# Masked graph attention: who issues the loads of the adjacency

## The chip, the cores and the metric

The kernel runs on one core of a Trainium2 chip. The metric is the device time of one execution in microseconds; lower is better. Where several runs are given, the median counts.

## The reference

With M = N = 6144 rows and D = 128:

```python
h = jnp.maximum(_layernorm(x, axis=-1), 0.0)
scores = jnp.where(adj > 0, h @ weight @ input.T, -2 ** 32 + 1)      # 6144 x 6144
out = x + softmax(scores / 0.07, axis=1) @ input
```

`adj` is a 6144 x 6144 int32 matrix of zeros and ones, 151 MB, and by far the largest input. The scores are wanted at nearly fp32 precision, so operands are split into a high and a low fp16 half.

## The kernel before

**Tiles and chunks.** The 6144 rows are worked on in 48 tiles of 128 rows. A tile's row of scores has 6144 columns. TensorE makes it in six chunks of 1024 columns (`score`, L816 to L824: six matmuls of 512 columns each, 36 per tile). VectorE masks each chunk with the codes of the adjacency (`mask`, L625 to L635), two chunks to each buffer of `codes`.

**The adjacency.** A tile's 128 x 6144 integers come in three loads of 128 x 2048 (1 MB each) into the three buffers of `adj_i`. GpSimd turns each buffer into codes by one pass (`convert`, L419 to L426): it waits for the load (`adj_in[c]`), and until the masks of the previous tile have read the buffer of `codes` that it will write (`masked`), and its end increments `coded`. The load of the next tile into the same buffer of `adj_i` may go out as soon as that pass has read it. SyncE issues it, after a wait on `coded`: `early_adj` (L317 to L322, L340) for tiles 1 and 2, and `next_adj` (L343 to L346) three times in each tile's step for tile t + 3. All of SyncE's transfers are on one DMA queue.

**The other things on SyncE.** In each tile's step SyncE also issues three pairs of transposes (`turn_d`, L324 to L336) that turn half of the exponentials, split by VectorE and ScalarE into fp16 halves, into `pT_dma`, from which TensorE multiplies (L859, L865, L867). A transpose waits for VectorE's `turn_freed` and for the product that last read its buffer. Then there are one load of x for the layernorm, one transpose of h (L368, after a wait on `h_split_done`), and one load of x for the residual. The order of these in a step is written out by hand, `next_adj(0)` behind the pair of c = 2, `next_adj(1)` behind the pair of c = 4, `next_adj(2)` behind the next tile's first pair.

**TensorE.** In a tile's step (L944 to L963) it runs three cycles; each turns two blocks of 512 columns through PSUM (`turn`, eight matmuls), makes two chunks of scores for tiles ahead, and multiplies four blocks of 512 with v (`product`, L848 to L869: eight matmuls each). The first tile's products wait for the low half of v, in four parts: block k needs part k // 3 (L850).

**GpSimd.** Its order is written out too: h of tiles 0 and 1; then, in the head (L453 to L466), the passes of tiles 0 to 2, mixed with the four parts of the low half of v (`v_lo_pool`, L428 to L437) and h of tile 2. In each tile's step t (L468 to L483): the pass for chunk 1 of tile t + 2, h of tile t + 3 and its split, the pass for chunk 2 of tile t + 2 and the one for chunk 0 of tile t + 3.

The steps of tiles 0 to 2 and of the last five are written out, the others are a loop over two tiles (`steps`, L287 to L295).

Of the kernel before, what the change touches and what calls it, by code (L numbers as in the profile page):

```python
# [5 lines left out]
def gnn_masked_attention_kernel(  # L6
# [93 lines left out]
    with ctx:  # L100
# [6 lines left out]
        def sem(name):  # L107
            return ctx.enter_context(nc.semaphore(name))
# [68 lines left out]
        x_ln_in = [sem(f"x_ln_in{i}") for i in range(2)]  # L177
        x_res_in = [sem(f"x_res_in{i}") for i in range(2)]
        adj_in = [sem(f"adj_in{i}") for i in range(CONVS)]
        stored = [sem(f"stored{i}") for i in range(2)]  # L180
        ident_zero = sem("ident_zero")
        ident_done = sem("ident_done")
# [116 lines left out]
        @block.sync  # L299
        def _(sp):  # L300
            def load_x(u, s):
                sp.dma_start(x_ln[:, s, :], x_v[u]).then_inc(x_ln_in[s], 16)

            def load_adj(u, c):
                sp.dma_start(adj_i[:, c, :], adj_v[u][:, c * CONV:(c + 1) * CONV]).then_inc(adj_in[c], 16)

            sp.dma_start(w[:, :], weight).then_inc(w_in, 16)
            for i in range(NODE_PARTS):
                blocks = slice(i * NODE_PART, (i + 1) * NODE_PART)
                sp.dma_start(nodes_raw[:, blocks, :], nodes_v[i]).then_inc(nodes_in[i], 16)  # L310
            for c in range(CONVS):
                load_adj(0, c)
            sp.dma_start(x_res[:, 0, :], x_v[0]).then_inc(x_res_in[0], 16)
            for u in range(2, 4):
                sp.wait_ge(h_done, u - 1)
                load_x(u, u % 2)
            def early_adj(n):  # L317
                sp.wait_ge(coded, n + 1)
                load_adj(n // CONVS + 1, n % CONVS)

            for n in range(2 * CONVS - 1):
                early_adj(n)  # L322

            def turn_d(u, c, g, count):  # L324
                d = c + g
                if count is None:
                    sp.wait_ge(split_done, d // 2 + 1)
                else:
                    sp.wait_ge(turn_freed, count)
                sp.sem_inc(sp_waited, 1)  # L330
                if not (isinstance(u, int) and u == 0):

                    sp.wait_ge(pv_done, u * TURNS + (2 * c + g + 1 - TURNS))
                sp.sem_inc(sp_waited, 1)
                sp.dma_start_transpose(pT_dma[:, d, :, :], split[:, d, :, :].rearrange("p s n -> p (s n)"))\  # L335
                    .then_inc(turned_in[d], 16)  # L336

            for g in range(2):
                turn_d(0, 0, g, g + 1)
            early_adj(2 * CONVS - 1)  # L340

            def step(t, par, at):
                def next_adj(c):  # L343
                    if has(at, 3):
                        sp.wait_ge(coded, t * CONVS + (2 * CONVS + c + 1))
                        load_adj(t + 3, c)  # L346

                for g in range(2):
                    turn_d(t, 2, g, late(at, 0, g) if at == LAST else evac(t, g - 2))
                next_adj(0)  # L350
                for g in range(2):
                    turn_d(t, 4, g, late(at, 1, g) if at == LAST else evac(t, 2 + g))
                next_adj(1)
                if has(at, 4):
                    sp.wait_ge(h_done, t + 3)
                    load_x(t + 4, par)
                if has(at, 1):
                    for g in range(2):
                        turn_d(t + 1, 0, g, late(at, 2, g) if at == LAST - 1 else evac(t, 6 + g))
                next_adj(2)  # L360
                if has(at, 3):

                    sp.wait_ge(scores_made, t * SCORES + 2 * SCORES)
                    sp.sem_inc(sp_waited, 1)
                    sp.wait_ge(h_split_done, t + (4 - H_TENSOR))
                    sp.sem_inc(sp_waited, 1)
                    s = 1 - par
                    sp.dma_start_transpose(hT[:, s, :, :], h_split[:, s, :, :].rearrange("p s n -> p (s n)"))\  # L368
                        .then_inc(hT_in[s], 16)
                if has(at, 1):  # L370
                    if at != 0:
                        sp.wait_ge(fin_done, t)
                    s = 1 - par
                    sp.dma_start(x_res[:, s, :], x_v[t + 1]).then_inc(x_res_in[s], 16)

            steps(sp, step)

        @block.gpsimd
        def _(pool):
# [37 lines left out]
                    .then_inc(h_split_done, 1)  # L417

            def convert(u, c):  # L419
                pool.wait_ge(adj_in[c], u * 16 + 16)  # L420
                if not (isinstance(u, int) and u == 0):

                    pool.wait_ge(masked, u * SCORES + (PER_CONV * (c + 1) - SCORES))
                pool.sem_inc(pool_waited, 1)
                nc.gpsimd.tensor_scalar(codes[:, c, :], adj_i[:, c, :], PRESENT_STEP, ABSENT, ALU.mult, ALU.add)\  # L425
                    .then_inc(coded, 1)  # L426

            def v_lo_pool(i):  # L428

# [578 lines left out]
```

## Time and profile before

| | us |
|---|---|
| median of 3 runs | 922.92 |
| lowest and highest | 921.91, 924.13 |
| the profiled execution, its time | 925.21 |
| its span in the profile | 923.4 |
| TensorE busy (PE) | 904.7, 98% |
| VectorE busy (DVE) | 809.6, 88% |
| ScalarE busy (ACT) | 738.4, 80% |
| GpSimd busy (POOL) | 419.4, 45% |
| granted TensorE clock, mean | 1.00 |
| moved by DMA | 242.46 MB, 263 GB/s |

Busy time is the union of the spans of an engine's instructions; matmul ends are modelled, so a busy TensorE need not be at its peak. The issuing of a transfer isn't counted as busy; such instructions are shown on the issuing engine's queue (SPq for SyncE, POOLq for GpSimd). An idle time in square brackets stands with what ended it.

### The profile page before, as it was taken

Reading aid. Unit: us, or ns where it says so; the run is one execution under the profiler, and the core shown is the slowest. Engines: PE = TensorE matmul, PEld = TensorE weight load, DVE = VectorE, ACT = ScalarE, POOL = GpSimd, SP = SyncE. Lnnn points to the kernel's source line nnn. Section 1 sums busy time; section 2 is a strip of 40 time slices with the busy share of each in tenths; the row PEclk is TensorE's granted clock in tenths of the full one; section 3 lists DMA queues with packets and bytes.
Section 4 is the critical chain, followed back from the end, with each engine's and each line's share of the span. In section 5 each row is a group of like instructions: output and inputs, shape, how many; then the busy total and the mean of one; then the engine's idle time right before and its main releaser. Section 6 shows DMA issues by size and latency. Waiting matters only on the chain.

```text
span 923.4 us, 25567 instructions
## 1 busy us (share of the span) xinstructions
PE 904.7 (98%) x7566; PEld 658.0 (71%) x7566; DVE 809.6 (88%) x1623; ACT 738.4 (80%) x1465; POOL 419.4 (45%) x447
## 2 busy tenths in 40 slices
PE   7999989999999999999999999999999999999997
PEld 4466767777777777777777777777777777777776
DVE  6988878988998899889988998898889888989985
ACT  5877778888888888888888888888888888888885
POOL 3974434444444444434543454445444544444402
DMA  9799999999999999999999999999999999999965
GB/s 317 242 252 282 272 229 273 283 267 277 274 271 264 279 273 272 263 275 274 273 270 267 274 275 274 271 266 273 275 275 259 275 276 276 260 275 270 272 108 100
DMA packets 364969, 242.46 MB, mean 263 GB/s; under 512 B 321808, under 2 KB 346512, under 8 KB 346512
## 3 DMA queue, kind: packets, MB, share of 16 engines
q1 hardware_dynamic: 357744, 238.87, 101.5%
q10 hardware_dynamic: 7200, 3.28, 1.4%
q8 instruction: 13, 0.21, 0.1%
q14 instruction: 12, 0.10, 0.1%
HBM read 160.50 MB, written 3.15 MB: 177 GB/s over the span
## 4 chain that ended last, share of the span: by engine, by line
PE 89%; DMA 4%; DVE 3%; SPq 2%; issue 1%; ACT 0%; DVEq 0%; ACTq 0%
PE ps_s L821 37%; PE ps_o L865 26%; PE ps_o L867 13%; PE ps_t L844 13%; DMA pT_dma<-split 3%; SPq L335 1%; DVE probs L631 1%; DMA nodes_raw<-in_L_gnn_input_dram 1%; SPq L310 1%; PE ps_t L884 1%; DVE split L660 0%; DVE pT_lo L654 0%; PE ps_o L884 0%; ACT yT_hi L544 0%; DVE pT_hi L650 0%
## 5 line engine op out<-in xcount | busy, mean ns | idle before, releaser
L425 POOL TENSOR_SCALAR codes<-adj_i 128x2048 uint32<-128x2048 int32 x144 | 273.8, 1902 | 292.7 <-DVE chunk_max L631 271.6
L631 DVE CUSTOM_DVE_ANT_0 probs<-ps_s,codes 128x1024 f32<-128x1024 f32 x288 | 351.5, 1221 | 50.2 <-PE ps_s L821 42.8
L821 PE MATMUL ps_s<-yT_hi,hT 128*128 128x512 f16 x1152 | 389.2, 379 | 0.9 <-DVE chunk_max L631 0.9
L539 ACT ACTIVATE pT_hi<-ps_t 128x512 f16<-128x512 f32 x281 | 167.8, 597 | 159.5 <-PE ps_t L844 159.4
L865 PE MATMUL ps_o<-v,pT_dma 128*128 128x256 f16 x1152 | 221.0, 273 | 6.7 <-DMA pT_dma<-split 6.7
L509 ACT ACTIVATE ps_t<-probs,neg_max,exp_scale 128x512 f32<-128x512 f32 x285 | 220.3, 773 | 5.3 <-DVE neg_max L641 4.0
L821 PE MATMUL ps_s<-yT_lo,hT 128*128 128x512 f16 x576 | 218.3, 379 | 0.0
L654 DVE TENSOR_TENSOR pT_lo<-ps_t,pT_hi 128x512 f16<-128x512 f32 x284 | 194.5, 685 | 26.1 <-ACT pT_hi L539 24.6
L865 PE MATMUL ps_o<-v,pT_hi 128*128 128x256 f16 x1152 | 205.8, 273 | 0.8 <-DVE pT_lo L654 0.8
L867 PE MATMUL ps_o<-v,pT_dma 128*128 128x128 f16 x1152 | 205.6, 219 | 0.0
L867 PE MATMUL ps_o<-v,pT_lo 128*128 128x128 f16 x1152 | 198.0, 219 | 0.0
L821 PEld LDWEIGHTS ps_s<-yT_hi,hT 128*128 128x128 f16 x1152 | 112.8, 98 | 107.9 <-DVE chunk_max L631 2.5
L660 DVE TENSOR_TENSOR split<-ps_t,split 128x512 f16<-128x512 f32 x285 | 182.5, 681 | 1.6 <-ACT split L519 1.5
L498 ACT ACTIVATE probs<-probs,neg_max,exp_scale 128x1024 f32<-128x1024 f32 x144 | 177.3, 1231 | 0.0
L844 PE MATMUL ps_t<-ident,probs 128*128 128x128 f32 x1136 | 172.3, 274 | 1.2 <-DVE split L660 1.1
L519 ACT ACTIVATE split<-ps_t 128x512 f16<-128x512 f32 x285 | 151.6, 581 | 0.0
L865 PEld LDWEIGHTS ps_o<-v,pT_dma 128*128 128x128 f16 x1152 | 112.6, 98 | 36.2 <-DMA pT_dma<-split 8.1
L865 PEld LDWEIGHTS ps_o<-v,pT_hi 128*128 128x128 f16 x1152 | 112.7, 98 | 29.2 <-DVE pT_lo L654 1.3
L867 PEld LDWEIGHTS ps_o<-v,pT_dma 128*128 128x128 f16 x1152 | 112.6, 98 | 17.1
L867 PEld LDWEIGHTS ps_o<-v,pT_lo 128*128 128x128 f16 x1152 | 112.7, 98 | 16.3
L844 PEld LDWEIGHTS ps_t<-ident,probs 128*128 128x128 f32 x1136 | 119.4, 140 | 5.3 <-DVE split L660 1.6
L821 PEld LDWEIGHTS ps_s<-yT_lo,hT 128*128 128x128 f16 x576 | 56.4, 98 | 36.9 <-issue 1.3
(78 smaller groups left out, 444.4 us busy)
## 6 DMA issues: line engine op xcount, KB each, us to landing
adj_i<-in_adj_dram SPq DMA_DIRECT2D x144, 1024.0 KB, 5.3
pT_dma<-split SPq DMA_TRANSPOSE x288, 3.5
nodes_raw<-in_L_gnn_input_dram SPq DMA_DIRECT2D x6, 512.0 KB, 7.1
x_res<-in_x_dram SPq DMA_DIRECT2D x48, 64.0 KB, 4.0
out_dram<-fin ACTq DMA_DIRECT2D x48, 64.0 KB, 2.6
x_ln<-in_x_dram SPq DMA_DIRECT2D x46, 64.0 KB, 4.9
hT<-h_split SPq DMA_TRANSPOSE x45, 5.1
x_ln<-in_x_dram ACTq DMA_DIRECT2D x2, 64.0 KB, 3.1
```

The costliest lines, as they stand in the source:

```text
L425: nc.gpsimd.tensor_scalar(codes[:, c, :], adj_i[:, c, :], PRESENT_STEP, ABSENT, ALU.mult, ALU.add)\
L498: nc.scalar.activation(part, part, ACT.Exp, bias=neg_max[:, s, :], scale=exp_scale[:, :], accum_out=chunk_sum[:, s, c // 2:c // 2 + 1]).th ...
L509: nc.scalar.activation(part if n is None else ps_t[n % BANKS][:, :], part, ACT.Exp, bias=neg_max[:, s, :], scale=exp_scale[:, :], accum_ou ...
L519: nc.scalar.activation(split[:, d, 0, :], ps_t[n % BANKS][:, :], ACT.Copy)\
L539: nc.scalar.activation(pT_hi[:, p % BANKS, :], turn_area(k, at), ACT.Copy).then_inc(hi_done, 1)
L631: nc.vector.tensor_tensor_reduce(out=probs[:, s, j * SCORE:(j + 1) * SCORE], in0=ps_s[j % 2][:, :], in1=codes[:, c, part * SCORE:(part + 1 ...
L654: nc.vector.tensor_tensor(pT_lo[:, p % BANKS, :], area, pT_hi[:, p % BANKS, :], ALU.subtract)\
L660: nc.vector.tensor_tensor(split[:, d, 1, :], ps_t[n % BANKS][:, :], split[:, d, 0, :], ALU.subtract).then_inc(turn_freed, 1)
L821: made = nc.tensor.matmul(ps_s[j % 2][:, q * 512:(q + 1) * 512], hT[:, s, part, :], y[:, cols], start=(part == 0 and y is yT_hi), stop=(pa ...
L844: made = nc.tensor.transpose(area[:, b * P:(b + 1) * P], probs[:, par, col:col + P], ident[:, :])
L865: nc.tensor.matmul(area[:, 0:2 * D], hi[b], v[:, blk, :, :].rearrange("p s d -> p (s d)"), start=(blk == 0), stop=(k == final and b == PER ...
L867: made = nc.tensor.matmul(area[:, 0:D], lo[b], v[:, blk, 0, :], start=False, stop=(k == final and b == PER_TURN - 1), skip_group_check=True)
```

## The change

GpSimd issues the load of the next tile's chunk itself, directly behind the pass that has read the buffer, after a wait until that pass has ended. SyncE issues only the three loads of tile 0, and its waits on `coded` are gone with the others. The loads that GpSimd issues have semaphores of their own (`adj_pool_in`), on which the passes of tiles 1 to 47 wait. The order of the rest is the same on both engines.

```diff
@@ GpSimd @@
             def convert(u, c):
-                pool.wait_ge(adj_in[c], u * 16 + 16)
+                if isinstance(u, int) and u == 0:
+                    pool.wait_ge(adj_in[c], 16)
+                else:
+                    pool.wait_ge(adj_pool_in[c], u * 16)
                 if not (isinstance(u, int) and u == 0):
 
                     pool.wait_ge(masked, u * SCORES + (PER_CONV * (c + 1) - SCORES))
                 pool.sem_inc(pool_waited, 1)
                 nc.gpsimd.tensor_scalar(codes[:, c, :], adj_i[:, c, :], PRESENT_STEP, ABSENT, ALU.mult, ALU.add)\
                     .then_inc(coded, 1)
+                if not (isinstance(u, int) and u + 1 >= TILES):
+
+                    pool.wait_ge(coded, u * CONVS + (c + 1))
+                    pool.sem_inc(pool_waited, 1)
+                    nc.gpsimd.dma_start(adj_i[:, c, :], adj_v[u + 1][:, c * CONV:(c + 1) * CONV])\
+                        .then_inc(adj_pool_in[c], 16)
@@ SyncE @@
-            def early_adj(n):
-                sp.wait_ge(coded, n + 1)
-                load_adj(n // CONVS + 1, n % CONVS)
-
-            for n in range(2 * CONVS - 1):
-                early_adj(n)
-
...
             for g in range(2):
                 turn_d(0, 0, g, g + 1)
-            early_adj(2 * CONVS - 1)
 
             def step(t, par, at):
-                def next_adj(c):
-                    if has(at, 3):
-                        sp.wait_ge(coded, t * CONVS + (2 * CONVS + c + 1))
-                        load_adj(t + 3, c)
-
                 for g in range(2):
                     turn_d(t, 2, g, late(at, 0, g) if at == LAST else evac(t, g - 2))
-                next_adj(0)
                 for g in range(2):
                     turn_d(t, 4, g, late(at, 1, g) if at == LAST else evac(t, 2 + g))
-                next_adj(1)
...
-                next_adj(2)
```

## Rows read from the trace of the kernel before

**Rows 1.** The page, part 1: busy time, share of the span, instructions.

```profile
PE 904.7 (98%) x7566; PEld 658.0 (71%) x7566; DVE 809.6 (88%) x1623; ACT 738.4 (80%) x1465; POOL 419.4 (45%) x447
```

**Rows 2.** Busy time by stretches of the span, with TensorE's granted clock and DMA.

```profile
core 0: us, PE busy (x) PEld busy (x) DVE busy (x) ACT busy (x) POOL busy (x), PEclk, DMA share, GB/s
...
20.00:40.00 20.00, 19.38 (x73) 7.86 (x72) 18.70 (x37) 15.15 (x21) 19.00 (x11) 1.00 0.70 261
40.00:60.00 20.00, 18.24 (x144) 12.19 (x143) 17.10 (x33) 16.50 (x35) 18.51 (x16) 1.00 1.08 268
...
80.00:100.00 20.00, 19.22 (x166) 13.95 (x164) 17.07 (x34) 15.53 (x32) 8.27 (x9) 1.00 1.19 262
...
300.00:500.00 200.00, 200.00 (x1701) 146.86 (x1700) 179.00 (x361) 163.89 (x329) 90.48 (x99) 1.00 1.05 272
...
900.00:923.40 23.40, 17.23 (x188) 15.11 (x186) 13.65 (x28) 13.59 (x28) 5.34 (x6) 1.00 0.52 99
```

**Rows 3.** Waits, whole span: waiter, releaser; us in total, times, longest us.

```profile
PE ps_o L865 <- DMA pT_dma<-split: 6.7, 7, 1.7
...
POOL h L404 <- POOL h_centred L397: 9.9, 48, 0.2
```

**Rows 4.** Timeline of TensorE: start us, us, instruction, [idle before, releaser].

```profile
57.48 0.27 PE L865 MATMUL ps_o<-v,pT_dma 128*128 128x256 f16 x1 [1.00 <-DMA pT_dma<-split]
...
58.58 0.27 PE L865 MATMUL ps_o<-v,pT_dma 128*128 128x256 f16 x1
...
70.03 0.28 PE L865 MATMUL ps_o<-v,pT_dma 128*128 128x256 f16 x1 [0.17 <-DMA pT_dma<-split]
...
84.32 0.28 PE L865 MATMUL ps_o<-v,pT_dma 128*128 128x256 f16 x1 [0.78 <-DMA pT_dma<-split]
...
127.62 0.28 PE L865 MATMUL ps_o<-v,pT_dma 128*128 128x256 f16 x1 [1.11 <-DMA pT_dma<-split]
...
135.65 0.28 PE L865 MATMUL ps_o<-v,pT_dma 128*128 128x256 f16 x1 [1.74 <-DMA pT_dma<-split]
```

**Rows 5.** Timeline of GpSimd in the head.

```profile
19.69 1.90 POOL L425 TENSOR_SCALAR codes<-adj_i 128x2048 uint32<-128x2048 int32 x1 [0.59 <-DMA adj_i<-in_adj_dram]
22.27 1.90 POOL L425 TENSOR_SCALAR codes<-adj_i 128x2048 uint32<-128x2048 int32 x1 [0.67 <-DMA adj_i<-in_adj_dram]
...
51.74 3.11 POOL L436 TENSOR_TENSOR v<-nodes_raw,v 128x1536 f16<-128x1536 f32 x1
```

**Rows 6.** Instructions of the tiles adj_i and pT_dma: ns min/median/max, first and last start.

```profile
L305 SPq DMA_DIRECT2D adj_i<-in_adj_dram x144: 328/367/1737, 9.0 to 872.4; - x144
L425 POOL TENSOR_SCALAR codes<-adj_i x144: 1897/1901/1925, 17.2 to 880.5; 128x2048 uint32<-128x2048 int32 x144
...
L335 SPq DMA_TRANSPOSE pT_dma<-split x288: 1231/1237/4418, 40.2 to 914.4; - x144
```

**Rows 7.** Timeline of GpSimd in the steady part.

```profile
507.43 1.90 POOL L425 TENSOR_SCALAR codes<-adj_i 128x2048 uint32<-128x2048 int32 x1 [4.22 <-DVE chunk_max L631]
...
515.72 1.90 POOL L425 TENSOR_SCALAR codes<-adj_i 128x2048 uint32<-128x2048 int32 x1
519.66 1.90 POOL L425 TENSOR_SCALAR codes<-adj_i 128x2048 uint32<-128x2048 int32 x1 [2.04 <-DVE chunk_max L631]
```

**Rows 8.** Timeline of SyncE's queue, at 126 us and in the steady part.

```profile
126.10 7.51 SPq L335 DMA_TRANSPOSE pT_dma<-split  x2
...
508.87 2.84 SPq L335 DMA_TRANSPOSE pT_dma<-split  x2
512.02 0.45 SPq L305 DMA_DIRECT2D adj_i<-in_adj_dram  x1
```

**Rows 9.** Timeline of TensorE in the steady part.

```profile
514.82 0.27 PE L865 MATMUL ps_o<-v,pT_dma 128*128 128x256 f16 x1
```

**Rows 10.** The page, parts 5 (groups) and 6 (issues: KB each, us to landing).

```profile
L631 DVE CUSTOM_DVE_ANT_0 probs<-ps_s,codes 128x1024 f32<-128x1024 f32 x288 | 351.5, 1221 | 50.2 <-PE ps_s L821 42.8
...
adj_i<-in_adj_dram SPq DMA_DIRECT2D x144, 1024.0 KB, 5.3
pT_dma<-split SPq DMA_TRANSPOSE x288, 3.5
```

More of the change, by code:

```diff
@@ L179, in gnn_masked_attention_kernel @@
         adj_in = [sem(f"adj_in{i}") for i in range(CONVS)]
+        adj_pool_in = [sem(f"adj_pool_in{i}") for i in range(CONVS)]
         stored = [sem(f"stored{i}") for i in range(2)]
```

## The prediction

> **What bounds the kernel now.** I read the busy table first: TensorE is at work for 904.7 of 923.4 us [rows 1]. The table by stretches then says where the other 18.7 us lie: from 300 to 500 us TensorE is busy for all of 200.00 us, at full granted clock, and the missing time is at the two ends [rows 2]. So in the steady part, nothing that the change does can gain; it can only lose there, by making TensorE wait. The gain can come from the first 140 us or the last 25. The waits name the candidate: TensorE waited 6.7 us in seven pieces for the transposes that SyncE issues (pT_dma) [rows 3]. Five of them are in the timeline: 1.00 us at 57.48, 0.17 at 70.03, 0.78 at 84.32, 1.11 at 127.62, 1.74 at 135.65 [rows 4]; the other two lie ahead of the first of these, and at the end of the run, when no adjacency is loaded any more.
>
> The second reading is the engine that gets the new work. Over the whole run GpSimd is only 45% busy [rows 1], which looks harmless. By stretches it is not: 19.00 of 20 us from 20 to 40, 18.51 of 20 from 40 to 60, and then 90.48 of 200 [rows 2]. In the head it has the passes of three tiles and the low halves of v to make, back to back, and it has 8.27 us of work from 80 to 100. An average would have hidden this.
>
> **The change, part by part.**
>
> *SyncE gives up 141 loads and their waits.* An issue there takes 0.37 us [rows 6], so some 1.1 us per tile come off its queue, together with its waits on `coded`. In the steady part this is worth nothing: its transposes wait for VectorE's split. The other effect is in the queue. SyncE's loads and transposes share one queue, and where a load has just gone in, the transposes behind it are slow: the pair at 126.10 took 7.51 us to issue, where an undisturbed one takes 2.84 [rows 8]. Off that queue, the 0.17 and 0.78 us at 70 and 84 us should go, 0.95 us. The waits at 127.62 and 135.65, 2.85 us together, come around that one long pair; the profile doesn't say whether the load ahead is its whole cause, and I count half, 1.4 us. The 1.00 us at 57.48 vanishes behind the delay worked out below. Gain: 2.4 us, with bounds of 0 and 3.8.
>
> *GpSimd gets, behind each pass with a next tile, a wait on its own pass and an issue.* The wait is the kind it already has: 9.9 us over 48 in `h`, 0.2 us each [rows 3]. The issue has no row, since GpSimd issues no transfer now. The nearest rows are SyncE's: 0.37 us for the very same load, and 1.24 us for a transpose, the longest issue there when nothing stands in its way [rows 6]. The bounds are 0.37 below and, above, one of GpSimd's own passes over a megabyte, 1.90 us [rows 6]. I take 1.24: the load's own row is another engine's, and between ends so far apart the value in the middle has a row of its own. With the wait that is 1.44 us for each pass.
>
> The Trainium skill speaks against the move in "DMA: Bandwidth & Descriptors", section "Specifications": a transfer issued by GpSimd takes about 1 us to its first byte, because a program writes its descriptors, and one from SyncE about 0.6 us. No row here shows it; taking 1.0 us for the issue instead of 1.24 would make the head's cost, worked out next, 4.6 us instead of 6.5.
>
> *What it costs in the head.* What waits for GpSimd there is, in order, the codes of tiles 0 to 2, h of tile 2, and the four parts of the low half of v. The tightest is the last part of v: GpSimd finishes it at 51.74 + 3.11 = 54.85 us [rows 5], and the first product that needs it, k = 9 of tile 0, starts at 58.58 [rows 4], so there are 3.73 us in hand. In GpSimd's order eight passes stand ahead of it (tile 0's three, tile 1's three, the first two of tile 2), each with an issue behind it now. GpSimd was idle before two of them, 0.59 and 0.67 us, waiting for tile 0's loads [rows 5], and that takes up 1.26 us. So the part comes 8 x 1.44 - 1.26 = 10.3 us later, at 65.1, and the product 10.3 - 3.73 = 6.5 us later. The earlier gates (codes of tile 1, h of tile 2, the third part of v for k = 6) are late by less and are steps on the way to the same 65.1, not additions. Behind it TensorE has nothing idle that could take the delay up [rows 2], so the whole run moves by it. SyncE, in its turn, is held by `h_split` of tile 3, which comes about 10 us later than before, and so reaches its next transposes about when their data is ready, since that has also moved by 6.5 us; I price that at nothing, and its cover is the same delay.
>
> *In the steady part GpSimd's extra work is covered.* A tile has 156 matmuls (36 for scores, 96 for products, 24 turns), and 1701 are in those 200 us [rows 2], so a tile takes 200 x 156 / 1701 = 18.3 us. Of that GpSimd is busy 90.48 x 18.3 / 200 = 8.3 us, and three issues with their waits add 3 x 1.44 = 4.3. The only two passes close together start at 515.72 and 519.66; the first ends at 517.62, its issue would at 519.06, and 2.04 us of idle time stood there [rows 7]. If the issue took over 1.8 us the second would slip a little, and its codes are for the next tile's step, at least a third of a tile (6 us) later. Cost: nothing.
>
> *The loads themselves move.* In the steady part, SyncE issues a load only after the transposes that stand ahead of it: the pass that starts at 507.43 ends at 509.33 [rows 7], but the load goes out at 512.02, behind the pair of 508.87 [rows 8]. Now it will go out at about 509.5 and flow from about 510.8, beside the second transpose. A load takes 5.3 us to land and a transpose 3.5 [rows 10]. This pair is used from 514.82 on [rows 9], 2.45 us after the first lands; the second is used one product and one turn, 1.1 us, later. I take zero, with the next rival as the upper end.
>
> Sum: +6.5 - 2.4 = +4.1 us. The profiled execution took 925.21 us (span 923.42); the median is 922.92, 0.25% below it. On the median this gives 927.0 us. A measurement of this kernel can tell about 0.2%, 1.85 us, from no change.
>
> **Rivals.**
>
> *The issue is cheap.* At 0.37 us, 8 x 0.57 - 1.26 = 3.3 us, less than the 3.73 in hand, so the head loses nothing. Then only the gain is left: 2.4 us, 920.5, at best 3.8, and 919.1. The two signs meet at about 0.62 + 2.4 / 8 = 0.92 us per pass, wait included. For it: SyncE does the same load in 0.37. Against it: it is another engine. Chance 0.22, of which a tenth ends within the 0.2%.
>
> *The steady part takes a new wait.* If a load that flows beside a transpose holds it up by its own full length, about 3 us, the pair at 508.87 comes 0.5 us too late for 514.82. At most two of the three pairs per tile can lie so, since GpSimd's passes and the pairs are spread differently over the tile. Where one of them stalls TensorE by 0.2 us in each of 44 tiles, the run gets 9 us longer, and 936 comes out. For it: 7.51 us for a pair in trouble [rows 8]. Against it: sharing is likely fairer than that, and the second transpose's later use. The point from which it decides is a delay of about 2.5 us. Chance 0.12. It makes the run slower on top of the head.
>
> *GpSimd is kept from its issue by VectorE.* If each issue had to sit out one of VectorE's long operations, 1.22 us [rows 10], a pass would cost 1.44 + 1.22 = 2.66 us and the head 8 x 2.66 - 5.0 = 16.3 us: about 937 with the gain. The operation reads one operand from PSUM (ps_s) and one from SBUF (codes) [rows 10]. The Trainium skill, "SBUF — State Buffer", section "Who interferes with whom", has this rule: GpSimd cannot write its descriptors while VectorE runs in a mode that takes both ports. By the same section an operation with one SBUF operand outside those modes does not take them, and no run here has tried it. Chance 0.05.
>
> *The change does nothing measurable,* because the issue's price falls between 0.6 and 0.9 us, and the head's loss and the queue's gain cancel: 8 x 0.8 - 5.0 - 2.4 = -1.0 to 8 x 1.1 - 5.0 - 2.4 = +1.4 us, or 921.9 to 924.3. Chance 0.10.
>
> **How the numbers follow.** The forecast, head later by 3 to 12 us, has 0.51; cheap issue 0.22; cancelled 0.10; steady wait 0.12; ports 0.05. Faster: 0.20. Within 0.2%: 0.02 + 0.10 and a little of the forecast's lower edge, 0.13. Slower: 0.67. The forecast's own range is the issue at 0.9 to 1.9 us: 8 x 2.1 - 5.0 = 11.8 us with no gain gives 934.7, 8 x 1.1 - 5.0 = 3.8 less the full 3.8 gives 922.9. For 8 in 10 the range must take in most of the cheap case and part of the steady wait: 919.5 to 936.
>
> **What would show it.** Right: GpSimd issues of about 1.2 us behind each pass; the last part of v done at about 65 us; TensorE idle for some 6 us between 40 and 60, ended by GpSimd's v or codes; the later waits for pT_dma shorter; full 200 of 200 us from 300 to 500. Wrong: the part of v done before 58 us, or an issue under 0.6 us; TensorE short of 200 us in the steady stretch with pT_dma as the releaser; or waits at 127 and 135 us that stay whole.

## The result, and the profile after

The changed kernel takes **1119.85 us** (median of 7 runs, 1107.76 to 1152.23), the kernel before 921.91 us beside it (7 runs, 921.13 to 924.13): a ratio of 1.209 (95% interval 1.207 to 1.211). Ratios here and below leave out runs more than 1.5% above the fastest of their kernel (here 1140.66 and 1152.23 us), so they can lie below the quotient of the medians (here 1.215), and where too few runs are left none is given. The forecast of 927.0 us had the direction and not the size; 1119.85 lies far outside 919.5 to 936. The profiled execution took 1152.23 us, span 1150.5, the longest of the seven: its rows say where the time goes, not to the microsecond how much.

The page, part 1 (columns as in [rows 1]), and from part 3 the queues: SyncE's is q1, GpSimd's q0 (packets, MB, share of the 16 engines' time).

```profile
PE 966.7 (84%) x7566; PEld 678.3 (59%) x7566; DVE 812.1 (71%) x1623; ACT 738.6 (64%) x1465; POOL 502.9 (44%) x588
...
q1 hardware_dynamic: 337440, 91.01, 54.3%
q0 software_dynamic: 20304, 147.86, 42.8%
```

VectorE and ScalarE are busy for as long as before. They, and TensorE, wait. Busy time by stretches, which answers [rows 2]:

```profile
core 0: us, PE busy (x) PEld busy (x) DVE busy (x) ACT busy (x) POOL busy (x), PEclk, DMA share, GB/s
20.00:40.00 20.00, 19.37 (x72) 7.78 (x71) 18.71 (x36) 15.15 (x21) 17.86 (x12) 1.00 0.70 243
40.00:60.00 20.00, 13.55 (x81) 8.12 (x78) 11.54 (x22) 10.79 (x23) 16.67 (x15) 0.83 1.05 184
80.00:100.00 20.00, 11.34 (x67) 7.36 (x66) 7.54 (x17) 4.97 (x10) 5.30 (x9) 0.66 0.94 170
300.00:500.00 200.00, 168.56 (x1334) 119.16 (x1335) 138.21 (x277) 127.46 (x256) 82.80 (x98) 0.93 1.00 211
500.00:700.00 200.00, 173.82 (x1397) 122.89 (x1395) 147.36 (x294) 134.10 (x268) 90.33 (x108) 0.96 0.99 223
```

TensorE is no longer full in the steady part: 168.56 of 200 us, and 1334 matmuls instead of 1701. A tile of 156 matmuls now takes 200 x 156 / 1334 = 23.4 us, where it took 18.3. Five microseconds a tile over some 44 tiles is 220 us, nearly all of the 227 us that the profiled execution lost. The DMA engines count as busy as before and move 211 instead of 272 GB/s. The waits, which answer [rows 3] (waiter, releaser; us in total, times, longest):

```profile
PE ps_o L859 <- DMA pT_dma<-split: 170.3, 64, 10.2
...
POOL adj_i L419 <- POOL codes L413: 98.9, 138, 0.8
```

Of TensorE's 6.7 us for the transposes 170.3 have become. The groups of the page (parts 5 and 6) and the transposes' row, beside [rows 6, 10]:

```profile
L419 POOL DMA_DIRECT2D adj_i<-in_adj_dram x141 | 84.3, 598 | 103.6 <-POOL codes L413 98.9
...
adj_i<-in_adj_dram POOLq DMA_DIRECT2D x141, 1024.0 KB, 7.2
pT_dma<-split SPq DMA_TRANSPOSE x288, 5.1
```

```profile
L329 SPq DMA_TRANSPOSE pT_dma<-split x288: 1230/1248/10650, 40.4 to 1141.5; - x144
```

The issue by GpSimd costs 0.60 us, and the wait for its own pass 98.9 / 138 = 0.72 us. A load takes 7.2 us to land instead of 5.3, a transpose 5.1 instead of 3.5, and a single transpose's issue up to 10.65. The timeline of the head and of one steady pair (the SPq row at 502.63 holds two pairs, the second from 508.45 on):

```profile
19.96 0.78 POOL L419 DMA_DIRECT2D adj_i<-in_adj_dram  x1 [0.67 <-DMA adj_i<-in_adj_dram]
...
49.88 0.37 PE L859 MATMUL ps_o<-v,pT_dma 128*128 128x256 f16 x1 [4.27 <-DMA pT_dma<-split]
...
61.12 3.09 POOL L430 TENSOR_TENSOR v<-nodes_raw,v 128x1536 f16<-128x1536 f32 x1
...
64.70 0.10 PEld L859 LDWEIGHTS ps_o<-v,pT_dma 128*128 128x128 f16 x1 [5.24 <-POOL v L430]
...
501.15 1.89 POOL L413 TENSOR_SCALAR codes<-adj_i 128x2048 uint32<-128x2048 int32 x1 [2.92 <-DVE chunk_max L625]
502.63 11.16 SPq L329 DMA_TRANSPOSE pT_dma<-split  x4
503.77 0.58 POOL L419 DMA_DIRECT2D adj_i<-in_adj_dram  x1 [0.73 <-POOL codes L413]
...
513.54 0.39 PE L859 MATMUL ps_o<-v,pT_dma 128*128 128x256 f16 x1 [3.75 <-DMA pT_dma<-split]
```

In the head the product comes as late as forecast: the last part of v ends at 61.12 + 3.09 = 64.21 us (forecast 65.1), and the product that needs it starts at 64.73 instead of 58.58, 6.15 us later (forecast 6.5). But v isn't all that it waited for. The chain (the page's part 4, in order of time) reaches it through one transpose, issued at 46.28 and landed at 64.59, 0.4 us after v:

```profile
46.28 18.31 DMA pT_dma<-split
```

So the product would have come as late with v ready in time. TensorE had waited 4.27 us for another transpose at 49.88 already, and it goes on losing behind the head's passes (11.34 of 20 us busy from 80 to 100, before 19.22). The steady part isn't as forecast at all: the first transpose of a pair goes in at 502.63, GpSimd's load 1.1 us behind it, and the second transpose at 504.45; in the chain that one takes 9.04 us, and TensorE's wait of 3.75 us at 513.54 ends with it:

```profile
504.45 9.04 DMA pT_dma<-split
```

### The profile page after: what moved, and what is told of

Read it like the earlier page. It is cut to its first block, busy times and chain, and to the rows that moved or that the text cites. A ratio compares the mean times of both kernels' runs of the same rounds, so it can differ in the third digit from the quotient of the medians.

```text
span 1150.5 us, 25730 instructions
## 1 busy us (share of the span) xinstructions
PE 966.7 (84%) x7566; PEld 678.3 (59%) x7566; DVE 812.1 (71%) x1623; ACT 738.6 (64%) x1465; POOL 502.9 (44%) x588
## 4 chain that ended last, share of the span: by engine, by line
PE 39%; DMA 39%; issue 6%; SPq 6%; DVE 6%; POOL 2%; DVEq 1%; ACT 0%; POOLq 0%
DMA pT_dma<-split 38%; PE ps_s L815 18%; PE ps_o L859 12%; PE ps_o L861 5%; SPq L329 5%; PE ps_t L838 4%; DVE split L654 3%; DVE fin_a L671 1%; DVE probs L625 1%; POOL codes L413 1%; DMA adj_i<-in_adj_dram 1%; SPq L311 1%; POOL v L430 1%; DVE pT_lo L648 0%; DVE fin L677 0%
## 5 line engine op out<-in xcount | busy, mean ns | idle before, releaser
L815 PE MATMUL ps_s<-yT_hi,hT 128*128 128x512 f16 x1152 | 409.6, 397 | 2.0 <-DVE chunk_max L625 2.0
L859 PE MATMUL ps_o<-v,pT_dma 128*128 128x256 f16 x1152 | 232.1, 282 | 170.5 <-DMA pT_dma<-split 170.3
L859 PEld LDWEIGHTS ps_o<-v,pT_dma 128*128 128x128 f16 x1152 | 115.5, 100 | 216.9 <-DMA pT_dma<-split 169.0
L815 PE MATMUL ps_s<-yT_lo,hT 128*128 128x512 f16 x576 | 229.6, 399 | 0.0
L859 PE MATMUL ps_o<-v,pT_hi 128*128 128x256 f16 x1152 | 218.7, 283 | 0.8 <-DVE pT_lo L648 0.8
L861 PE MATMUL ps_o<-v,pT_dma 128*128 128x128 f16 x1152 | 215.6, 225 | 0.0
L861 PE MATMUL ps_o<-v,pT_lo 128*128 128x128 f16 x1152 | 208.5, 225 | 0.0
L859 PEld LDWEIGHTS ps_o<-v,pT_hi 128*128 128x128 f16 x1152 | 117.8, 102 | 36.7 <-issue 5.8
L419 POOL DMA_DIRECT2D adj_i<-in_adj_dram x141 | 84.3, 598 | 103.6 <-POOL codes L413 98.9
L861 PEld LDWEIGHTS ps_o<-v,pT_lo 128*128 128x128 f16 x1152 | 117.3, 102 | 19.3 <-issue 5.2
L861 PEld LDWEIGHTS ps_o<-v,pT_dma 128*128 128x128 f16 x1152 | 115.9, 101 | 16.5
```

Of the source, the lines that this page charges most:

```text
L815: made = nc.tensor.matmul(ps_s[j % 2][:, q * 512:(q + 1) * 512], hT[:, s, part, :], y[:, cols], start=(part == 0 and y is yT_hi), stop=(pa ...
L859: nc.tensor.matmul(area[:, 0:2 * D], hi[b], v[:, blk, :, :].rearrange("p s d -> p (s d)"), start=(blk == 0), stop=(k == final and b == PER ...
L861: made = nc.tensor.matmul(area[:, 0:D], lo[b], v[:, blk, 0, :], start=False, stop=(k == final and b == PER_TURN - 1), skip_group_check=True)
```

## Experiments

**The theory.** In SyncE's one queue a load that is issued behind a pair of transposes can't touch it. On another queue it shares the DMA engines with the transposes that are still to run, holds them for its own length, and is itself drawn out. A tile has some 6 us from a pair's issue to its first use (508.87 to 514.82, [rows 8, 9]). **Rivals:** the head; GpSimd's own time; the queue that software fills; the small size of the transposes' packets against the load's.

### Head or steady part, bytes or instructions

pool_head lets GpSimd issue the loads of tiles 1 and 2 alone; pool_steady those from tile 3 on alone; pool_narrow and pool_half are pool_steady with 256 and 1024 of a load's 2048 columns (they leave the rest of the adjacency stale, but run the same instructions).

```diff
@@ pool_head, against before @@
+                if isinstance(u, int) and u < 2:
+                    pool.wait_ge(coded, u * CONVS + (c + 1))
+                    nc.gpsimd.dma_start(adj_i[:, c, :], adj_v[u + 1][:, c * CONV:(c + 1) * CONV])\
@@ pool_steady, against before @@
+                by_pool = c in (0, 1, 2)
+                if by_pool and not (isinstance(u, int) and (u < 2 or u + 1 >= TILES)):
@@ pool_narrow, against pool_steady (pool_half: 1024 for 256) @@
-                    nc.gpsimd.dma_start(adj_i[:, c, :], adj_v[u + 1][:, c * CONV:(c + 1) * CONV])\
+                    nc.gpsimd.dma_start(adj_i[:, c, 0:256], adj_v[u + 1][:, c * CONV:c * CONV + 256])\
```

> Only the six loads of tiles 1 and 2 are GpSimd's, issued behind the passes as in the changed kernel; from tile 3 on SyncE issues them as before. By the prediction's own sum, with the 1.31 us per pass that the changed kernel's trace shows (0.73 of wait and 0.58 of issue) and six issues ahead of the last part of v instead of eight, the product of k = 9 comes 6 x 1.31 - 1.26 - 3.73 = 2.9 us later: 925 to 928 us. If the head is what makes the changed kernel slow (a late start that the steady part never gets over): 1000 us and more.

> The reverse: SyncE issues the loads of tiles 0 to 2 as before, GpSimd all others. P (phase: the steady part is slow because GpSimd's loads flow while pairs of transposes are under way): 1080 to 1150 us, nearly all of the loss. H (the head's late start does it): under 950 us.

> As pool_steady, but each of GpSimd's loads moves only 256 of the 2048 columns (rows of 1 KB, 128 KB in all); the other columns keep what tile 2's load left, so from tile 3 on most of the adjacency is stale. Same issues at the same places. P (the bytes that flow beside the transposes): the harm goes, 915 to 930 us. If GpSimd's issue or its descriptors as such hold up VectorE, SyncE or the DMA engines: still over 1000 us.

> From tile 3 on GpSimd issues all loads at the changed kernel's places, each of 1024 of the 2048 columns (rows of 4 KB, 512 KB in all); the other half of each chunk stays stale. A load then flows about 1.6 us instead of 3.2. With 2.4 us in hand for a pair, P says that most of the harm goes: 920 to 960 us. A cost by the byte alone would give half the loss of the whole loads, some 1020.

| | us, median (range) | ratio (95%) |
|---|---|---|
| pool_head | 928.77 (928.62 to 930.67) | 1.0065 (1.0044 to 1.0087) |
| pool_steady | 1129.89 (1089.6 to 1157.36) | |
| pool_narrow | 921.44 (919.9 to 922.27) | 0.9981 (0.9968 to 0.9994) |
| pool_half | 961.11 (956.47 to 961.95) | 1.0398 (1.0365 to 1.0432) |

The head costs 6.1 us for six issues, just above the 925 to 928 us expected; the steady part alone loses as much as the whole change (207 us on the median, 167 to 235 from run to run). pool_narrow has every instruction and every wait of pool_steady, and it costs nothing: so it isn't GpSimd's time, and the loss comes with the bytes, more than in proportion (an eighth of them nothing, half 38 us, all 207).

Nor is it mainly GpSimd's time that pool_head pays for. Its chain runs through a transpose, issued at 45.63 between two of GpSimd's loads:

```profile
45.63 15.29 DMA pT_dma<-split
...
59.10 3.10 POOL L440 TENSOR_TENSOR v<-nodes_raw,v 128x1536 f16<-128x1536 f32 x1
```

TensorE waits for transposes there, 5.52 us at 51.88 and 1.67 at 61.05, and for the last part of v, ready at 62.20, only 0.2. The steady stretch, from 300 to 500 us, of pool_narrow, then of pool_steady:

```profile
300.00:500.00 200.00, 200.00 (x1703) 146.99 (x1702) 179.42 (x362) 163.96 (x328) 110.02 (x131) 1.00 0.58 121
```

```profile
300.00:500.00 200.00, 177.95 (x1466) 127.18 (x1467) 152.35 (x305) 139.39 (x280) 93.38 (x112) 0.98 1.00 234
```

### The size of the packets

A row of a load is one packet of 8192 bytes. pool_2k is the changed kernel with adj_i padded, so that each row lands in four pieces of 2048 bytes.

```diff
-        adj_i = sb("adj_i", [P, CONVS, CONV], int32)
+        adj_i = sb("adj_i", [P, CONVS, 4, 520], int32)
-                    nc.gpsimd.dma_start(adj_i[:, c, :], adj_v[u + 1][:, c * CONV:(c + 1) * CONV])\
+                    nc.gpsimd.dma_start(adj_i[:, c, :, 0:512], adj_v[u + 1][:, c * CONV:(c + 1) * CONV].rearrange("p (h n) -> p h n", h=4))\
...
```

SyncE's loads of tile 0 and GpSimd's pass are changed likewise.

> The changed kernel with adj_i padded every 512 columns, so that each load moves rows of 2 KB instead of 8 KB, four times as many; same bytes, same times of issue. Q (turns between two queues, packet by packet): a transpose packet waits behind a quarter of the bytes, so the transposes crawl less: 930 to 1040 us. T (too early): unchanged, 1080 to 1150. S (GpSimd's descriptors): four times as many of them, 1120 us and more. GpSimd's issue, 0.58 us for 128 rows, should grow, to 1 to 2.3 us.

The packets did not become what was meant. The queues of pool_2k:

```profile
q0 software_dynamic: 38352, 147.86, 46.1%
```

Less 16 tiny ones for each of the 141 loads, that is 256 packets for a load instead of 128: two of 4096 bytes for each row, half the size and not a quarter. The run takes 1031.71 us (1022.83 to 1037.86), ratio 1.1134 (1.1062 to 1.1207), although the longer issue (0.80 us) adds to the head. Packets of half the size take 88 us of the 198 away, as one expects where queues take turns by packets; with the size of the packets the pass and the issue changed a little too, so this alone doesn't prove it. The same count tells of pool_half and pool_narrow that their loads go in 128 and in 32 packets of 4096 bytes, so against pool_steady the size of the packets changed with the bytes, and the two aren't told apart there.

### Which of the three loads

pool_chunk0, pool_chunk1 and pool_chunk2 leave one load of each tile to GpSimd from tile 3 on, and the two others to SyncE.

```diff
-                by_pool = c in (0, 1, 2)
+                by_pool = c in (1,)
+                next_adj(0)
...
+                next_adj(2)
```

> From tile 3 on GpSimd issues only the load of chunk 2, SyncE those of chunks 0 and 1 as before. In the trace of the kernel before, the pass of chunk 2 ends at 517.62; with 0.73 us of wait and 2.2 us from the issue to the first packets it would flow from about 520.5 to 523.5, on top of the pair that SyncE issues at 520.34. P (phase): this load alone does much of the harm, 960 to 1080 us. If it is the number of GpSimd's transfers that counts, a third of the loss: 980 to 1000. If another queue is harmless as such: under 930.

> As the run with chunk 2 alone, but GpSimd issues only the load of chunk 1. Its pass ends at 509.33 in the kernel before, so its load would flow from about 512.3 to 515.5: SyncE issued the same load at 512.02, between two pairs. P (phase): this one is harmless, 920 to 932 us, although it is on GpSimd's queue like chunk 2's, which gave 982.

> GpSimd issues only the load of chunk 0. Its pass ends at 521.56, so the load would flow from about 524.5 to 527.7, with its tail on the pair that follows one tile later at 527.2; in SyncE's order the next load then stands behind that pair, not beside this one. P: little harm, 920 to 945 us. If every load by GpSimd costs alike: 980 as for chunk 2.

pool_chunk2 takes 981.67 us (972.93 to 983.48; ratio 1.0618, 1.0557 to 1.0679), pool_chunk0 996.55 (976.07 to 1011.17, over the 920 to 945 expected), pool_chunk1 1090.67 (1082.02 to 1091.27; ratio 1.1788, 1.1734 to 1.1842). The last was expected to be harmless, and by itself loses 168 us. (The three losses add up to some 300 us, more than the 207 of pool_steady, so they are not shares of it.) Its timeline:

```profile
510.07 1.90 POOL L429 TENSOR_SCALAR codes<-adj_i 128x2048 uint32<-128x2048 int32 x1 [5.21 <-DVE chunk_max L640]
511.50 2.83 SPq L336 DMA_TRANSPOSE pT_dma<-split  x2
512.73 0.64 POOL L434 DMA_DIRECT2D adj_i<-in_adj_dram  x1 [0.76 <-POOL codes L429]
```

The pass of chunk 1 ends just as a pair goes in, so that load falls on it: from 100 us on, 41 of its 42 issues lie between those of a pair's two transposes. What the packets do, counted from the same trace by half microseconds, some of them left out here (packets of 256 bytes are the transposes', of 8192 the load's; a transpose has 1024 of them and a load 128):

```
pool_chunk1   from us   q1, 256 B        q0, 8192 B (mean us each)
              513.0     418              -
              513.5     361              -
              514.0     12               8  (1.36)
              514.5     0                3  (1.22)
              515.5     3                12 (0.54)
              516.5     15               18 (0.47)
              517.5     21               19 (0.38)
              518.5     138              10 (0.32)
              520.0     424              -
before        511.0     437              -
              512.5     484              -
              515.5     -                25 (0.33, on q1)
```

The first transpose runs at some 400 packets in half a microsecond. From 514.0, when the load's packets start, the second gets about as many packets as the load does or fewer, for 4 us; from 516 on it is about one of 256 bytes for one of 8192. It runs on at speed only at 520, when the load is through; the load took 5.5 us. In the kernel before the pair is through by about 513.1 and the load flows behind it.

### Order kept in another way: GpSimd waits for the pair

pool_late (all loads, over the changed kernel), steady_late (over pool_steady) and chunk1_late (over pool_chunk1) let GpSimd wait until the pair has landed before it issues.

```diff
+                    if pair is not None:
+                        pool.wait_ge(turned_in[pair[0]], pair[1])
+                        pool.sem_inc(pool_waited, 1)
...
+                        convert(t + 2, 1, (3, t * 16 + 16))
```

> GpSimd issues the loads as in the changed kernel, but in the steps each waits in addition until the pair of transposes that is under way has landed, so that it goes out at about the time at which SyncE issued it before. T (too early): all is as before, under 935 us. Q (another queue): the front of a load no longer meets a pair, but its tail meets the next one, which in one queue would stand behind it: 970 to 1110 us. S (GpSimd's descriptors): 1050 us and more.

> As the run in which GpSimd issues all loads from tile 3 on (1129.89 us), but each waits until the pair under way has landed. With the changed kernel's head the same waits gave 1020.68, with GpSimd's order slipped (a wait of 6.4 us per tile, passes late, two loads in a row). If that slip comes from the head's delay: 920 to 940 us here. If it comes from the waits themselves, since GpSimd's next passes and h queue up behind them: 990 to 1040 again.

> As the run with chunk 1 alone (1090.67 us), but GpSimd waits, before it issues that load, until the second transpose of the pair under way has landed (an order that SyncE's one queue gave for free). In the run before, the load's first packets flowed at 514.0, half a microsecond ahead of the second transpose's, and that transpose then took until 521. O (order: a transpose that is still to run when a load starts on another queue is held for the whole load): nearly all of the 168 us comes back, 920 to 940 us. If a load on GpSimd's queue is slow or harmful as such: 1000 us and more.

All three gain, and none gets back to 922, though chunk1_late was expected at 920 to 940: pool_late 1020.68 us (1001.44 to 1027.79), steady_late 1010.08 (1004.78 to 1037.99; ratio 1.0905, 1.0869 to 1.0941), chunk1_late 986.56 (974.94 to 989.94; ratio 1.0629, 1.0549 to 1.0709), 104 us below pool_chunk1. What remains in chunk1_late:

```profile
510.71 0.34 SPq L306 DMA_DIRECT2D adj_i<-in_adj_dram  x1
...
513.12 0.63 POOL L437 DMA_DIRECT2D adj_i<-in_adj_dram  x1 [5.07 <-DMA pT_dma<-split]
513.40 5.61 SPq L336 DMA_TRANSPOSE pT_dma<-split  x2
```

Two loads go in ahead of one pair, within 2.4 us, and the pair's part of the chain is 6.83 us, over the 6 that it has. And a wait on GpSimd holds all that is queued behind it (h, the next passes). The waits of steady_late by releaser:

```profile
POOL adj_i L430 <- DMA pT_dma<-split: 360.3, 60, 10.3
...
PE ps_o L870 <- DMA pT_dma<-split: 89.1, 55, 8.3
```

### The same order against the same phase, with one queue and with two

Phase here means when a load is issued, seen from the pair of transposes. sp_behind is the control: all loads by SyncE, one behind each pair, some a third of a tile earlier than before. sp_beside puts two of them between the transposes of a pair. one_now is sp_behind with chunk 1's load given to GpSimd, right behind its pass; one_late adds the wait for the pair.

```diff
@@ sp_behind, against before (sp_beside: the first and the last inside the pair's loop, behind g == 0) @@
+                if has(at, 3):
+                    adj_behind(t + 3, 1, t * CONVS + (2 * CONVS + 2))
...
+                if has(at, 3):
+                    adj_behind(t + 3, 2, t * CONVS + (2 * CONVS + 3))
...
+                    if has(at, 4):
+                        adj_behind(t + 4, 0, t * CONVS + (3 * CONVS + 1))
@@ one_now, against sp_behind @@
-                if has(at, 3):
-                    adj_behind(t + 3, 1, t * CONVS + (2 * CONVS + 2))
+                by_pool = c == 1
```

> SyncE issues all loads in its one queue, but as early as the changed kernel does: between the two transposes of a pair, or right behind them. T (too early): 1050 us and more, with TensorE waiting for pT_dma. Q (another queue) and S (GpSimd's descriptors): near the kernel before, 920 to 940 us, as the second transpose comes at most a load's 3 us later and 2 to 4 us are in hand.

> As the run in which SyncE issued each load between the two transposes of a pair (1003.36 us), but each stands behind its pair: the same loads, in the same thirds of a tile as the changed kernel's, one after each pair, in one queue. O (order: a transpose that is still to run when a load starts is held): 918 to 930 us. If having the load a third of a tile earlier than before hurts by itself: 960 and more. It is also the control for the next two.

> As sp_behind, but the load of chunk 1 is GpSimd's, directly behind its pass and with no further wait, one load for each pair as in the changed kernel (the earlier run with chunk 1 alone had two loads between two pairs, one of SyncE's and one of GpSimd's). Its first packets come about half a microsecond before the second transpose of the pair has run. O: that transpose is held for the whole load, 1000 to 1110 us. If the earlier run's loss came from the two loads in a row: under 950.

> As one_now, with one wait more: GpSimd issues the load only when the pair has landed, so there are one load for each pair and no transpose still to run. O: near the control, 918 to 945 us. If a load in GpSimd's queue is harmful as such, or the wait itself costs GpSimd too much: 970 and more.

| | us, median (range) | ratio (95%) |
|---|---|---|
| sp_behind | 927.87 (926.84 to 928.6) | 1.0071 (1.0054 to 1.0087) |
| sp_beside | 1003.36 (1002.89 to 1008.71) | 1.0878 (1.0834 to 1.0922) |
| one_now | 1089.57 (1084.49 to 1093.08) | 1.1804 (1.1765 to 1.1843) |
| one_late | 1047.11 (1038.63 to 1051.43) | 1.1343 (1.1278 to 1.1407) |

In one queue, behind the pair, the loads cost nothing in the steady part even a third of a tile earlier: 200.00 of 200 us from 300 to 500 in sp_behind. (Its 5.8 us lie in the head: TensorE is busy for 15.88 us from 40 to 60, before for 18.24.) Ahead of the second transpose, still in one queue, the loads cost 81 us, which neither theory had: so some harm is done without a second queue, by a load that gets ahead of a pair's second transpose. And the move of one load per tile to another queue costs 162 us over the control. one_late was expected between 918 and 945 us and missed. In its timeline GpSimd's load doesn't lie on a pair, but GpSimd waits 8.24 us before the issue, so that h and the passes come late, and with them hT and SyncE's own loads, which hold the transposes behind them. That this is the whole of its loss is read from the trace, not tried:

```profile
500.28 5.95 SPq L336 DMA_TRANSPOSE pT_dma<-split  x4
502.88 0.39 PE L836 MATMUL ps_s<-yT_hi,hT 128*128 128x512 f16 x1 [0.35 <-DMA hT<-h_split]
505.85 0.64 POOL L440 DMA_DIRECT2D adj_i<-in_adj_dram  x1 [8.24 <-DMA pT_dma<-split]
```

### GpSimd's queue or any queue

act_queue and act_from3 give ScalarE's queue all steady loads (act_from3 from tile 6 on alone), at places of its own order; act_now is sp_behind with only chunk 1's load moved, to where one_now has it.

```diff
@@ act_queue @@
+                    if z == 0 and has(at, 3):
+                        act_load(t + 3, 1, t * CONVS + (2 * CONVS + 2))
+                    if z == 1 and has(at, 3):
+                        act_load(t + 3, 2, t * CONVS + (2 * CONVS + 3))
+                    if z == 2 and has(at, 4):
+                        act_load(t + 4, 0, t * CONVS + (3 * CONVS + 1))
@@ act_from3 @@
+                    if z == 0 and at not in (0, 1, 2) and has(at, 3):
@@ act_now, against sp_behind (SyncE's load of chunk 1 taken out) @@
+                    if z == 0 and has(at, 3):
+                        act.wait_ge(coded, t * CONVS + (2 * CONVS + 2))
+                        act.dma_start(adj_i[:, 1, :], adj_v[t + 3][:, CONV:2 * CONV]).then_inc(adj_in[1], 16)
```

> ScalarE instead of GpSimd issues the steady part's loads on its own queue, shortly behind the pass that read the buffer (the head's loads are SyncE's again). Three theories. Q: the loads hurt because they are on another queue than the transposes, so that an engine's load packets and transpose packets take turns; by whom they are issued does not matter: 1050 to 1150 us, with the transposes' issue in fours of about 10 us and TensorE waiting 100 us and more for pT_dma. S: only loads whose descriptors GpSimd writes hurt: under 935 us. T: the loads hurt because they go out some 2.5 us sooner, beside a pair of transposes: also 1050 to 1150 here.

> As the run with ScalarE's queue, but SyncE also keeps the loads that it issued in the first three steps, and ScalarE begins with tile 6's; that run's one long wait, 5.06 us at 56.75, came in the first step. P: the steady part stayed full there with the loads on another queue than the transposes, since each flows between two groups of transposes, so this one is level with the kernel before, 919 to 928 us. If another queue costs by itself: 930 and more.

> sp_behind again (927.87 us) with SyncE's load of chunk 1 taken away and issued by ScalarE instead, for tile 3 on, right behind its store of the output, at about 512.3 us of the step where one_now (1089.57 us) had GpSimd issue the same load at about 511.7. No engine waits any longer than for its own pass, and all other loads stay in SyncE's queue behind their pairs. If what harms is any second queue at this phase, the load's packets take turns with those of the two transposes still under way, and the run comes out at 1000 to 1100 us, with TensorE below 190 of 200 us from 300 to 500 and pT_dma as the releaser. If what harms is that GpSimd's transfers are served differently (a queue that software fills), the load lets the transposes through and the run stays at 920 to 940 us with 198 us or more in that stretch. Between 940 and 1000: both have a part.

act_queue takes 937.49 us (927.71 to 956.01), act_from3 937.13 (928.06 to 942.05; ratio 1.0106, 1.0044 to 1.0169). From 300 to 500 us both have TensorE at 200.00: the second queue does no harm where its load starts in the gap, 1.7 us ahead of the next pair, as in act_queue, where 110 of the load's 128 packets have started by 506.0, when those of the pair begin:

```profile
502.10 0.34 ACTq L568 DMA_DIRECT2D adj_i<-in_adj_dram  x1
...
503.82 4.51 SPq L335 DMA_TRANSPOSE pT_dma<-split  x2
```

act_from3 was expected at 919 to 928; some runs of both are slower still, and their spread stays unexplained. act_now takes **1231.28 us** (1223.72 to 1242.59), ratio 1.3318 (1.3239 to 1.3397), above the 1000 to 1100 expected:

```profile
510.47 12.51 SPq L335 DMA_TRANSPOSE pT_dma<-split  x4
...
512.40 0.35 ACTq L589 DMA_DIRECT2D adj_i<-in_adj_dram  x1
...
523.34 0.40 PE L870 MATMUL ps_o<-v,pT_dma 128*128 128x256 f16 x1 [5.71 <-DMA pT_dma<-split]
```

So it is not GpSimd's queue: a hardware queue at nearly the same phase does the same, and worse. (ScalarE issues some 0.4 us behind the second transpose, GpSimd in one_now 0.4 us ahead of it, and GpSimd's first packets take 0.4 us longer to come.) In its packets (same count as above) the second transpose gets 15, 7 and 23 packets in the three microseconds from 514, and the load 8, 7 and 22, where it alone has some 50. The first of the load's packets take 2.1 to 2.6 us on average, the longest 5.57. Why both nearly stand still there isn't settled.

No version beat the kernel before clearly; pool_narrow, 0.2% below it, leaves seven eighths of the steady loads out.

## Why the prediction was wrong

**What bounds the kernel: right.** With TensorE at 200.00 of 200 us the steady part could only lose.

**SyncE gives up its loads, gain 2.4 us: not seen by itself.** The nearest is pool_narrow: waits for pT_dma of 3.6 us in 3 pieces instead of 6.7 in 7, and 1.2 us less on the median, within the bounds of 0 and 3.8.

**GpSimd's price, 1.44 us a pass: near.** It is 0.58 to 0.60 for the issue and 0.59 for the wait in the head, 1.18 together, and 0.60 + 0.72 = 1.32 over the run. The issue was taken too high (1.24) and the wait too low (0.2, from waits of h on its own engine). The Trainium skill, "DMA: Bandwidth & Descriptors", section "Specifications", has the first byte at about 1 us for a transfer of GpSimd's and 0.6 for one of SyncE's or ScalarE's. The order is the same here, the times are longer: the first packet comes 1.6 us after the issue starts in pool_chunk1 (GpSimd) and 1.0 in act_queue (ScalarE), in the median.

**The head, +6.5 us: the number came out, the cause only in part, and that is luck.** The last part of v was 0.9 us off, and the product 0.35 us off. But the product's own transpose landed later still (64.59 against 64.21), held up by what the failed step below left out; each of the two would have given about this delay by itself. Where only the head was changed they come apart: for pool_head the same sum gives 2.9 us, TensorE waits 0.2 us for v, and the run still loses 6.1, with waits of 5.52 and 1.67 us for transposes and 1.32 for a mask. No run has GpSimd's issues in the head without their bytes.

**In the steady part GpSimd's work is covered: right** (pool_narrow). The rival of the ports has fallen too: GpSimd's issues take 578 ns at the least and in the median and 777 at the most, with VectorE busy for 71% of the span; none had to sit out an operation of 1.22 us.

**"The loads themselves move", taken at zero: this step failed.** It saw all that was needed: the load would go in at 509.5 instead of 512.02 and flow beside the second transpose. But it then let the transfer cost nothing, and the rival that priced it allowed a delay of 3 us, a stall of 0.2 us a tile and 9 us in all, with a chance of 0.12. Measured are 5 us a tile. Three things were wrong in it. First, the load was read as late by accident ("SyncE issues a load only after the transposes that stand ahead of it") when that order is the transposes' protection (sp_behind, 200.00 of 200 us). Second, "sharing is likely fairer than that": it is about one packet for one, which gives a transpose of 1024 packets beside a load of 128 next to nothing until the load has ended. Third, the load's length was taken as 3 us, and it is drawn out as well (5.5 us of packets in pool_chunk1, 7.2 us to landing in the changed kernel). So a transpose that took 3.5 us to land takes 9.04 in the example; from a pair's issue to its first use there are 6, and TensorE waits 3.75. The head shows the same: 18.31 and 15.29 us for a transpose.

The Trainium skill has a rule for it, in "DMA: Bandwidth & Descriptors", section "Queues, rings and completion order": a DMA engine takes its queues in turn and drains a whole packet, typically of some 9 to 17 descriptors, from one before it switches. The taking in turns agrees with the counts here; the unit doesn't, since they show single records, one of 256 bytes for one of 8192. Its section "Issuing engines are not separate DMA queues" says that issuing from several engines saves only the engine's own time; here the same load from another engine made the run longer by 162 and 303 us (one_now and act_now over sp_behind), as the order against the transposes is lost.

**Why so much.** A stall costs more than its own length. After such a stall TensorE is at half clock for a time, 1.2 instead of 2.4 GHz, as the stretches around the wait that ended at 513.54 show (the granted clock is the third number from the right):

```profile
512.00:513.00 1.00, 0.00 (x0) 0.00 (x0) 0.00 (x0) 1.00 (x3) 0.64 (x1) 0.92 1.02 220
513.00:514.00 1.00, 0.46 (x3) 0.39 (x4) 0.00 (x0) 0.06 (x1) 0.00 (x0) 0.50 1.67 258
514.00:515.00 1.00, 1.00 (x8) 0.76 (x6) 0.00 (x0) 0.00 (x0) 0.00 (x0) 0.50 0.62 172
...
516.00:517.00 1.00, 1.00 (x7) 0.51 (x6) 0.00 (x0) 0.00 (x0) 0.00 (x0) 0.87 0.95 380
```

The mean from 300 to 500 is 0.93. An estimate of the shares there: at full clock the 1334 matmuls would take 200 x 1334 / 1701 = 156.9 us, and they took 168.56. So of the 43.1 us lost in 200, 31.4 are idle time and 11.7 are the lower clock.

## What to carry to other kernels

Before a load is moved to another engine, ask what its place in the old queue protected. In this kernel's one queue order worked as a priority: behind the pair a load cost nothing. On two queues the transfer of few large packets took the DMA engines from that of many small ones, from GpSimd and from ScalarE alike, and the few microseconds of slack that TensorE had were gone. A forecast that comes out for one product doesn't show its cause either: look whether a second thing arrived at the same time. Price the overlap with the whole length of the large transfer, or place the load so that it starts in a gap; a wait on the issuing engine that restores the order holds everything queued behind it (steady_late, 1010.08 us).

## What the runs showed of the hardware

- A load (128 packets of 8192 bytes) and a transpose (1024 of 256 bytes) on two queues progress about packet for packet, some 15 to 20 of each in half a microsecond (pool_chunk1), where a transpose alone has 400 to 480.
- Near the end of such a load, packets of the transposes take 0.41 to 0.69 us each instead of 0.018. In the changed kernel the DMA engines are busy from 510 to 512 us, and 64 packets of 256 bytes and 5 of 8192 go through. It looks as if the whole transpose ran at the pace of the one engine that has a load packet left; the trace doesn't name the engines, so this is a reading and not shown.
- A wait of GpSimd for the end of its own pass takes 0.59 to 0.8 us in the changed kernel, where one for a short operation took 0.2 [rows 3].
- Of a row that lands in four pieces of 2048 bytes, GpSimd's queue makes two packets of 4096 (pool_2k, 38352 packets on q0). SyncE's, for the loads of tile 0 there, keeps them at 2048 (1536 packets for three loads).
- The load on ScalarE's hardware queue harms more than the same on GpSimd's (1231.28 and 1089.57 us).
